# Cross-attention loop: keys, x, queries and mask rows prepared two batches early, long jobs on odd visits of three units

## The reference

```python
x = x + _L1_xattn_ref(_layernorm(x, axis=-1), ctx_1024, ctx_1024, mask_BxSxS2_if1, Wq, bq, Wk, bk, Wv, bv, Wo, bo)

def _L1_xattn_ref(Q, K, V, mask, Wq, bq, Wk, bk, Wv, bv, Wo, bo):
    q = _split_heads(Q @ Wq.T + bq)
    k = _split_heads(K @ Wk.T + bk)
    v = _split_heads(V @ Wv.T + bv)
    scores = jnp.einsum('bhqd,bhkd->bhqk', q, k) / jnp.sqrt(jnp.float32(D_K))
    scores = jnp.where(mask[:, None, :, :] == 0, NEG_INF, scores)
    attn = jax.nn.softmax(scores, axis=-1)
    out = jnp.einsum('bhqk,bhkd->bhqd', attn, v)
    ...
    return out @ Wo.T + bo
```

## Time and profile before

| | |
|---|---|
| time, median of 3 runs | 2673.34 us (2672.87 to 2675.73) |
| the profiled execution | 2665.32 us, span 2663.6 us |
| cross stage, set-up | 998 to 1074 us |
| cross stage, eight batches | 1074 to 1678 us |
| TensorE busy over the span | 2122.1 us (80%) |
| VectorE, ScalarE, GpSimd busy | 56%, 35%, 31% |
| mean granted TensorE clock | 0.937 |

### The profile page before, as it was taken

One profiled execution on the slowest core, in us unless ns is written; L12 is line 12 of the kernel. 1 busy time (PEld: TensorE's weight loads), 2 busy tenths in 40 slices (PEclk: granted clock), 3 DMA queues, 4 the chain that ended last, 5 costly groups with the idle time before them and its releaser, 6 DMA issues. The chain is left out here.

```text
span 2663.6 us, 37640 instructions
## 1 busy us (share of the span) xinstructions
PE 2122.1 (80%) x11952; PEld 1389.3 (52%) x11961; DVE 1484.3 (56%) x2297; ACT 926.3 (35%) x1539; POOL 836.8 (31%) x753
## 2 busy tenths in 40 slices
PE   2340899999999505889888888838999999999997
PEld 1340899999999502333333333614545545554554
DVE  7820454545554344567666666544656656656655
ACT  2410333333333200455555555312333333333332
POOL 0067553435550362122212222011323323333232
PEclk9999999999999856899999999669999999999999
DMA  3162332333322332232232232324233223223322
GB/s 126 63 243 101 111 115 79 117 122 110 122 78 65 109 88 88 89 102 89 82 104 84 87 98 86 118 53 95 58 73 86 65 68 86 69 61 86 76 56 64
DMA packets 149071, 244.68 MB, mean 92 GB/s; under 512 B 22502, under 2 KB 71310, under 8 KB 146698
## 3 DMA queue, kind: packets, MB, share of 16 engines
q1 hardware_dynamic: 109762, 164.07, 21.9%
q0 software_dynamic: 11104, 44.06, 4.8%
q10 hardware_dynamic: 28160, 35.99, 4.2%
HBM read 120.48 MB, written 67.04 MB: 70 GB/s over the span
## 5 line engine op out<-in xcount | busy, mean ns | idle before, releaser
L1108 DVE TENSOR_REDUCE ca_negmax<-ca_na 128x2 f32<-128x1024 f32 x272 | 332.4, 1224 | 153.6 <-PE ca_na L901 153.6
L1020 ACT ACTIVATE ca_pr<-ca_st 128x512 f32<-128x512 f32 x512 | 278.9, 597 | 206.6 <-PE ca_st L915 205.6
L901 PE MATMUL ca_na<-ca_k_stack,ca_q_stack 64*128 64x512 f32 x544 | 222.7, 489 | 59.0 <-DMA ca_q_stack<-ca_zrow 55.6
L592 DVE TENSOR_TENSOR ex_h<-ex_up,ex_sg 128x512 f32<-128x512 f32 x136 | 94.1, 692 | 306.8 <-ACT ex_sg L555 197.4
L1706 DVE TENSOR_REDUCE sa_negmax<-sa_na 128x1 f32<-128x512 f32 x272 | 182.7, 674 | 130.8 <-PE sa_na L1527 126.5
L915 PE MATMUL ca_st<-ca_q_stack,ca_k_stack 64*128 64x512 f32 x512 | 210.6, 473 | 29.5 <-ACT ca_pr L1020 26.5
L515 PE MATMUL ex_gp<-ex_xp,moe_gu_p 128*128 128x256 f32 x1632 | 221.8, 286 | 1.4 <-DVE ex_xp L578 1.4
L515 PE MATMUL ex_up<-ex_xp,moe_gu_p 128*128 128x256 f32 x1632 | 218.4, 284 | 0.0
L528 PE MATMUL ex_yp<-moe_dn_p,ex_hp 128*128 128x256 f32 x1632 | 208.8, 286 | 11.3 <-DVE ex_hp L582 11.3
L515 PEld LDWEIGHTS ex_gp<-ex_xp,moe_gu_p 128*128 128x128 f32 x1632 | 206.1, 193 | 2.4 <-DVE ex_xp L578 1.8
L528 PEld LDWEIGHTS ex_yp<-moe_dn_p,ex_hp 128*128 128x128 f32 x1632 | 198.8, 192 | 15.2 <-DVE ex_hp L582 15.2
(11 more groups left out here) (261 smaller groups left out, 3798.1 us busy)
## 6 DMA issues: line engine op xcount, KB each, us to landing
sa_q<-sa_qh SPq DMA_DIRECT2D x140, 128.0 KB
sa_k<-sa_kh SPq DMA_DIRECT2D x140, 128.0 KB
ex_raw_m<-masks ACTq DMA_DIRECT2D x34, 512.0 KB, 3.8
moe_gu_raw<-gateupT POOLq DMA_DIRECT2D x8, 2048.0 KB, 8.2
ca_q_stack<-q_parts SPq DMA_DIRECT2D x216, 64.0 KB
ca_k_stack<-k_parts SPq DMA_DIRECT2D x216, 64.0 KB
expert_rows<-rt_zeros SPq DMA_DIRECT2D x20, 512.0 KB, 15.9
k_parts<-ca_kp SPq DMA_DIRECT2D x9, 1024.0 KB, 4.3
```

What stands on the lines that cost most here:

```text
L901: last = pe.matmul(na[r % 2][:, i, :], q_stack[g][rows, i, t * P:(t + 1) * P], k_stack[g][rows, i, :], start=not masked, stop=True)
L1020: act.activation(pr[:, s // HG % 2, s % HG, :], st[s % 2][:, :], ACT.Exp, scale=DK ** -0.5).then_inc(exp_done, 1)
L1108: dve.tensor_reduce(negmax[:, g % 2, 1 - r % 2, :, r // 2], na[r % 2][:, :, :], AX.X, ALU.max, negate=True).then_inc(max_done, 1)
```

## The change

k, xT, q and rv are now made in batch b for batch b+2, v still for batch b+1 (`batch`). The stores of both k and q move to the end of SyncE's loop body, behind the loads of stack 3 and a wait for all four stacks. `ctxT` serves v alone and is loaded at the head of the body; k gets its own copy of the context, `ctxK`, loaded there too. The transposed mask has three buffers. Stack 0 waits only for unit 0 and for stores issued a batch earlier. The long jobs stand on odd visits of units 1 to 3 (three, three and two), none in unit 0. Before the loop the list `FIRST` makes k, x, q and rv of batch 0 and of batch 1, the latter behind v1.

```diff
-        JOBS = [("m", 0, 0), ("k0", 0, 1), ("n0", 0, 2), ("k1", 0, 3), ("xT0", 0, 4), ("xT1", 0, 5), ("rv", 0, 6), ("q0", 0, 7),
+        JOBS = [("m", 0, 0), ("n0", 0, 3), ("xT0", 0, 4), ("t0", 0, 5), ("xT1", 0, 6), ("t1", 0, 7),
+                ("m", 1, 0), ("v0", 1, 1), ("n1", 1, 2), ("o0", 1, 3), ("v1", 1, 5), ("rv", 1, 7),
...
-        FIRST = ["k0", "k1", "xT0", "xT1", "rv", "q0", "q1", "v0", "v1", "m"]
+        FIRST = [("k0", 0), ("k1", 0), ("xT0", 0), ("xT1", 0), ("rv", 0), ("q0", 0), ("q1", 0), ("v0", 0), ("v1", 0),
+                 ("xT0", 1), ("xT1", 1), ("rv", 1), ("k0", 1), ("k1", 1), ("q0", 1), ("q1", 1), ("m", 0)]
...
+        def batch(name, b):
+            return b + 1 if name[0] == "v" else b + 2
...
+            load_context(sp, io, ctxK, ck_in, 1)
+            load_bias_T(0, 0)
+            load_bias_T(1, 1)
             load_bias(0, 0)
...
             for g in range(G):
                 load_stack(g)
-            sp.wait_ge(misc_full, FIRST.index("v1") + 1)
-            load_context(sp, io, ctxT, ctx_in, 1)
+            for g in range(G):
+                sp.wait_ge(stack_in[g], LOAD)
+            store(kp, k_parts, misc_free, k_stored, first("k1", 1) + 1)
+            store(qp, q_parts, qp_ready, q_stored, 2 * KC)
             send_rows(0, 0)
             with sp.Fori(0, B) as b:
                 sp.wait_ge(exp_done, b * G * SLOTS + 2)
-                for g in range(G):
-                    sp.wait_ge(stack_in[g], b * LOAD + LOAD)
-                load_bias(nxt(b), (b + 1) % 2)
+                load_bias((b + 1) % B, (b + 1) % 2)
+                load_bias_T((b + 2) % B, (b + 2) % 3)
+                load_context(sp, io, ctxT, ctx_in, (b + 1) % B)
+                load_context(sp, io, ctxK, ck_in, (b + 2) % B)
                 send_rows(1, b * G + 1)
-                store(kp, k_parts, misc_free, k_stored, b * nj + (nf + number("k1") + 1))
-                send_rows(2, b * G + 2)
-                store(qp, q_parts, qp_ready, q_stored, b * KC + 2 * KC)
                 for g in range(G):
                     sp.wait_ge(exp_done, b * G * SLOTS + ((g + 1) * SLOTS + 2))
...
                     load_stack(g)
-                    if g == 1:
-                        send_rows(3, b * G + 3)
-                    if g == 2:
-                        load_context(sp, io, ctxT, ctx_in, (b + 2) % B)
-                        send_rows(0, b * G + 4)
+                    if g < G - 1:
+                        send_rows((g + 2) % G, b * G + (g + 2))
+                for g in range(G):
+                    sp.wait_ge(stack_in[g], b * LOAD + 2 * LOAD)
+                store(kp, k_parts, misc_free, k_stored, b * nj + (nf + number("k1") + 1))
+                store(qp, q_parts, qp_ready, q_stored, b * KC + 3 * KC)
...
@@ prepare (TensorE)
                 if name == "rv":
-                    pe.wait_ge(nbT_in, b * 16 + 16)
+                    pe.wait_ge(nbT_in, 32 if isinstance(b, int) else b * 16 + 16)
...
+                    now = isinstance(b, int) and b == 0
+                    if now:
+                        pe.wait_ge(ctx_in, 16)
+                    else:
+                        pe.wait_ge(ck_in, b * 16)
...
                 else:
+                    pe.wait_ge(ctx_in, b * 16 + 16)
...
@@ ScalarE, loop
+                        for n, name in jobs_at(g, r):
+                            if name[0] in "kxmt":
+                                evacuate(b * nj + (nf + n), name, batch(name, b))
                         if r == 0:
                             take(u, b * nj + nf + (number(f"n{g - 1}") + 1 if g else 0))
-                        for n, name in jobs_at(g, r):
-                            if name[0] in "kxmt":
-                                evacuate(b * nj + (nf + n), name, b + 1)
...
@@ GpSimd, loop
                     if g == 1:
-                        split_q(1, b * nj + (nf + number("q1")), b + 1)
                         add_bias(b)
-                    if g == 0:
-                        split_q(0, b * nj + (nf + number("q0")), b + 1)
-                    for i in {2: (0, 1), 3: (2,)}.get(g, ()):
-                        move_values(i, u + (G - g + i), b * nj + (nf + number("v1")))
+                    if g:
+                        move_values(g - 1, u + G - 1, b * nj + (nf + number("v1")))
+                    if g == 3:
+                        for c in range(KC):
+                            split_q(c, b * nj + (nf + number(f"q{c}")), b + 2)
...
@@ VectorE
+                if (name, b) == ("xT0", 1):
+                    normalise(1, 1)
...
-                        if (g, r) == (0, 1):
-                            normalise(b + 1, (b + 1) % B)
+                        if (g, r) == (0, 0):
+                            normalise(b + 2, (b + 2) % B)
```

More of the change, by code:

```diff
@@ L716, in cross_attention @@
         set_up = m.sem("set_up")
[L717 removed]
+        nb_in, nbT_in, ck_in = m.sem("nb_in"), m.sem("nbT_in"), m.sem("ck_in")
         xn_ready = m.sem("xn_ready")
@@ L751, in number, with first @@
             return next(n for n, j in enumerate(JOBS) if j[0] == name)
-        def nxt(b):
-            return b + 1 if isinstance(b, int) else (b + 1) % B
+        def first(name, b):
+            return FIRST.index((name, b))
+        def batch(name, b):
+            return b + 1 if name[0] == "v" else b + 2
         @block.sync
@@ L867, in prepare @@
                 if name == "rv":
-                    pe.wait_ge(nbT_in, b * 16 + 16)
+                    pe.wait_ge(nbT_in, 32 if isinstance(b, int) else b * 16 + 16)
                     for t in range(TB):
-                        last = pe.matmul(misc[:, :], tiny16[:, :], nbT[:, b % 2, t, :], start=(t == 0), stop=(t == TB - 1))
+                        last = pe.matmul(misc[:, :], tiny16[:, :], nbT[:, b % 3, t, :], start=(t == 0), stop=(t == TB - 1))
                 elif name[0] == "k":
-                    pe.wait_ge(ctx_in, b * 16 + 16)
+                    now = isinstance(b, int) and b == 0
[3 more added lines that the diff above has]
+                        pe.wait_ge(ck_in, b * 16)
                     for i in range(KC):
-                        last = pe.matmul(misc[:, :], wk[:, i, c * P:(c + 1) * P], ctxT[:, i, :], start=(i == 0), stop=(i == KC - 1))
+                        last = pe.matmul(misc[:, :], wk[:, i, c * P:(c + 1) * P], (ctxT if now else ctxK)[:, i, :], start=(i == 0), stop=(i == KC - 1))
                 elif name[0] == "x":
@@ L958, in all_units @@
                                 else:
-                                    prepare(job, name, b + 1)
+                                    prepare(job, name, batch(name, b))
             pe.wait_ge(w_in, 16 * 8)
-            for n, name in enumerate(FIRST[:-1]):
-                if n == 0:
-                    pe.wait_ge(set_up, SETUP)
-                prepare(n, name, 0)
+            pe.wait_ge(set_up, SETUP)
+            for n, (name, b) in enumerate(FIRST[:-1]):
+                prepare(n, name, b)
             for t in range(TB - 1):
@@ L1075, in _ @@
             for c in range(KC):
-                split_q(c, FIRST.index(f"q{c}"), 0)
+                split_q(c, first(f"q{c}", 0), 0)
             for g in range(G - 1):
-                move_values(g, g, FIRST.index("v1"))
+                move_values(g, g, first("v1", 0))
+            for c in range(KC):
+                split_q(c, first(f"q{c}", 1), 1)
             split_rows(nf - 1, 0)
```

27 lines of the change are left out of this document (16 added, 11 removed), and 5 rows, old and new, of the table JOBS.

## The result

The changed kernel takes 2690.57 us (median of 7 runs, 2684.43 to 2692.99) where the kernel before takes 2675.40 beside it (7 runs, 2668.72 to 2679.33): a ratio of 1.0057 with the interval 1.0043 to 1.0071, some 15 us slower. Forecast was no change (2673). The changed kernel's profiled execution has a span of 2690.4 us against 2663.6.

The account below looks back on a forecast made before the run. TensorE's cross loop was taken as the bound, with waits for late stacks; -7.7 - 12.2 + 16.4 + 3.5 = 0.0 us on the profiled 2665.3, whose median stands 8.0 above: 2673 us, no change; range 2635 to 2694.

Parts of the forecast that it names:

- (a): Cross loop, unit 2: stack 0 needs no fresh store, so its wait and the slow clock behind go, 8.4 us a batch.
- (b): Jobs in new places, without late transfers: units of 15.0, 17.35, 16.85 and 15.1 us, sum 64.3; places worth 2.4 a batch.
- (c): SP's queue: unit 1's rows behind 4.19 MB land at +22.3; batch 74.05 against 75.15, -7.7 us over batches 1 to 7.
- the 0.35 us: Unit 0's end: time from the last bulk byte at +21.95 to the rows landed with their completion at +22.3.
- The bounds (+20.5 to +23.8): Range for the rows' landing after unit 0's start: batch 72.2 to 75.6 us, batches 1 to 7 together -21 to +3.
- The estimate by the fit of the Trainium skill: 2.0 us plus bytes over 436 GB/s: 4.19 MB in 9.6 us, not 11.75, making the kernel 15 us faster; not used.
- (d): Batch 0 of the cross loop: no wait for rows, 66.0 us after against 78.2 before, -12.2 us.
- (e): Set-up before the loop: added jobs of batch 1, mostly at half clock, start the loop 16.4 us later, bounds 11 and 20.
- (f): The end: SP's last work includes both stores and their landing, 17.2 us against 13.7, +3.5.
- (C): Rival, chance 0.18: backlog flows slower, rows land past +23.4; at 300 GB/s +24.8, batch 76.55, whole 2694 us.
- (B): Rival, chance 0.15: rows overtake the bulk, landing at +17.3; batch 67.6 to 70 us, whole 2628 to 2645.
- The prediction's signs: Right: seven waits of 6 to 8 us for rows at unit 1's start; wrong: 2 to 3 (B), over 9 (C), none.

Follow-up runs that it names:

- e2_rows_ctx_first: Changed kernel with unit 1's rows issued first at a batch's head, ctxT right behind, then stack wait, both stores and other loads: 2599.18 us, ratio 0.9731 to before.
- e1_rows_first: Changed kernel with unit 1's rows issued first at a batch's head, then stack wait, both stores and the four loads: 2645.01 us, ratio 0.9905 to before.
- e13_hold_stack: Changed kernel with stack 0's fourteen loads held back until unit 1's rows have landed: 2678.44 us, ratio 1.0008 to before.
- e3: Changed kernel without the load of nb (512 KB) in the loop: 2670.65 us, ratio 1.0002 to before.
- e4_rows_act: Changed kernel with unit 1's four row transfers issued from ScalarE's queue in visit 3 of unit 0, bulk left on SyncE's: 2636.76 us, ratio 0.9870 to before.
- e12: Changed kernel without the load of ctxK in the loop (524 KB): 2671.80 us, ratio 1.0010 to before.
- e10_stores_rows: Changed kernel with batch head ordered stack wait, k and q stores, unit 1's rows, then the four loads: 2639.54 us, ratio 0.9887 to before.
- e6_loads_rows_stores: Changed kernel with batch head ordered four loads, unit 1's rows, then stack wait and both stores: 2616.08 us, ratio 0.9801 to before.
- e8_loads_then_stores: Changed kernel with batch head ordered stack wait, four loads, both stores, unit 1's rows last: 2671.92 us, ratio 1.0009 to before.

## Why the prediction was wrong

(a) *The late stack goes, 8.4 us a batch.* Right: no wait for a stack in 1170 to 1690, and unit 2 is 16.92 at clock 1.00. Batch 0 has no late rows, and there the gain of this and of the new places of the jobs stands alone: 78.4 to 66.3.

(b) *Units of 15.0, 17.35, 16.85, 15.1, sum 64.3.* Right: 64.2 to 65.2 in batches 1 to 6 of e2_rows_ctx_first, though unit 0 takes 16.1 in three of them (see the last section). In the changed kernel unit 1 takes 18.5 to 20.0 (forecast 17.35 + 2.45 = 19.8 with the slow clock after the wait), units 2 and 3 16.9 and 14.9.

(c) *The rows queue behind 4.19 MB and land at +22.3.* This is the term that failed. That the rows stand behind the bulk holds: their packets move at +22.0, and e1_rows_first takes the wait away by their place. The landing was off by 26.0 - 22.3 = 3.7 us. The last bulk byte was forecast for +21.95, and e13_hold_stack shows it, but for a few packets, at +22.2. The step that failed is the 0.35 us from there to PE's start. It is 1.6 when nothing else is queued, and 3.8 as the kernel was: the stack 0 loads, which my sum didn't hold at all, are worth the 2.2 us between. No row stood behind the 0.35, and one could have been read: in the trace of the kernel before, the rows of unit 1 take 1.2 us from the end of their last packet to the last step of their semaphore. With 1.6 the landing is +23.55 and the whole some 9 us more, about 2682 (an estimate). Units 1 to 3 gave back 0.5 and 0.2, so a batch came 3.1 dearer than forecast, and seven 21.7. The bounds (+20.5 to +23.8) took in the first of the two errors only. I took bytes over rate as the time of the last small transfer; the rate says when the bulk has flowed, and the row's landing is a term of its own.

The estimate by the fit of the Trainium skill ("DMA: Bandwidth & Descriptors", "Anatomy of one DMA") was misread beside it: 9.6 us is the bytes' part alone, and with the 2.0 us that the fit adds it is 11.6, as good as the 11.75 and not 15 us faster in all.

(d) *Batch 0, -12.2.* -12.1.

(e) *Set-up, +16.4, bounds 11 and 20.* +11.3, at the lower bound. The order of the added jobs was right, their clock was not. PE in the set-up of the changed kernel, with the earlier trace rows beside it:

```profile
1054.22 3.78 PE L893 MATMUL ca_misc<-ca_ctxK,cross_wk 128*128 128x512 f32 x4 [0.79 <-DVE ca_rv L1139]
1059.63 1.98 PE L893 MATMUL ca_misc<-ca_ctxK,cross_wk 128*128 128x512 f32 x4 [1.63 <-DVE ca_kp L1135]
1063.25 1.98 PE L900 MATMUL ca_misc<-ca_xT,cross_wq 128*128 128x512 f32 x4 [1.63 <-DVE ca_kp L1135]
1066.08 1.98 PE L900 MATMUL ca_misc<-ca_xT,cross_wq 128*128 128x512 f32 x4 [0.85 <-DVE ca_qf L1143]
```

Only k0 ran at the half clock (3.78 us), k1, q0 and q1 at the full one (1.98). From the end of v1 to the last values it is 25.0 us where the prediction had 28.2: 3.2 of the 5.1 us of the miss. Another 1.2 lie ahead of it, since batch 0's jobs (k0 to v1) took 29.7 us and not the 30.9 of the kernel before, as its half-speed stretches fell on other jobs, and 0.7 behind it, in the scores. Part of this is chance: the same set-up code takes 75.4 to 79.5 us in e3, e4, e12 and e13, where the changed kernel's profile has 77.6. By luck this miss hid a quarter of what (c) cost.

(f) *The end, +3.5.* +2.5.

Of the rivals, (C) is the one that came: a backlog that lands past +23.4. Its batch of 76.55 and its 2694 are near the 77.1 and 2690.6 measured, by luck: it had all bytes go at 300 GB/s, and they didn't. (By its own terms it lands at 9.3 + 0.9 + 14.0 + 0.35 = +24.5, and not at +24.8.) The chance of 0.18 was too low for it, since the forecast's own margin to the cross-over was 1.1 us, with a completion time that was read from no row. (B), rows that overtake the bulk, is refuted for one queue; with two, one row transfer overtook the stores in three batches of e4_rows_act.

The prediction's signs called waits of 6 to 8 us right and over 9 (C); they were 9.2 to 11.7.

## What to carry over

When a change makes an engine's operands earlier, look at the queue behind which the next small, urgent transfer stands, count the bytes ahead of it, and ask whether each of them is as urgent. Here the change gained 8.4 us a batch at one wait and lost more at another, by four 4 KB transfers behind 4.19 MB; sending the urgent ones first (rows, then ctxT, then stores and the rest) gives 2599 us without touching a single job of the engines. Give a small transfer behind bulk the time of the bytes plus one to two microseconds, and two more where loads like the stack's are issued right behind it: so it was here.

## What the runs showed of the hardware

- Stack loads issued behind the rows on the same queue delayed TensorE's release by 2.2 us (26.0 to 23.8, e13_hold_stack) and made its time uneven (25.4 to 26.5 against 23.64 to 23.87). Most of it lies behind the rows' data: from their last packet to the last step of their semaphore it took 2.4 to 3.5 us in the three kernels with stack 0's loads right behind, and 0.9 to 1.5 us in five kernels with stores, bulk loads or nothing there. The stack's loads are 64 KB each, in packets of 2 KB; such a packet took 205 ns on the mean (1259.6 to 1263 in the changed kernel), where one of the bulk of the same size took 90 (1255.1 to 1259). They moved at 133 to 172 GB/s with a full DMA share (1 us windows behind the bulk in e2_rows_ctx_first and e10_stores_rows) where the bulk moves at 380. Why they are slow, and why the rows' semaphore waits for them, is not shown; the traces don't tell the sixteen engines apart.
- Where stores give way to loads in one queue (the changed kernel and e13_hold_stack, after some 2 MB), two windows of 1 us fall to 184 to 244 GB/s, at a cost of 0.9 us. From loads to stores e6_loads_rows_stores shows nothing (381, 399 and 414 GB/s). The low windows inside the loads of e8_loads_then_stores are not explained.
- A 4 KB row transfer on ScalarE's queue passed stores queued on SP's: its packets moved at +11.5 to +12.1 while these flowed at 348 to 393 GB/s from +9.9 on, where without them they moved at +10.2 (e4_rows_act, batches 1, 2 and 5 against 3, 4, 6 and 7).
- Unit 0 without a long job is not always at full clock although TensorE waits for nothing long: in e2_rows_ctx_first it takes 14.8 us in four of seven batches and 16.1 in the other three. Parts of such a unit 0 (batch 3) and of one at full clock (batch 2), in the columns of the earlier trace rows:

```profile
1279.51:1283.51 4.00, 3.18 (x17) 1.24 (x17) 3.77 (x7) 3.83 (x8) 1.36 (x3) 1.00 0.36 93
1283.51:1288.51 5.00, 4.88 (x22) 1.94 (x24) 2.86 (x3) 2.71 (x6) 1.51 (x5) 0.66 0.31 86
1215.15:1219.15 4.00, 3.18 (x17) 1.24 (x17) 3.77 (x7) 3.83 (x8) 1.36 (x3) 1.00 0.37 97
1219.15:1224.15 5.00, 4.88 (x32) 1.86 (x32) 4.19 (x6) 3.73 (x8) 1.51 (x5) 1.00 0.31 83
```

  In batch 3 TensorE is busy 3.18 us of 4.00, and the granted clock falls to 0.66 over the next 5 us. The last two rows are the same stretches of batch 2: the same 3.18 us busy, and the clock stays at 1.00. So what TensorE did just before does not tell the two apart, and the cause is open. It costs 1.3 us a time, 4 in all. Whether a long job moved back into unit 0 would keep the clock up was not tried.
- From the rows' last packet to the last step of their semaphore it took 0.4 us where the four transfers stood alone (e1_rows_first, e2_rows_ctx_first), and 1.2 us in the kernel before, where they moved together behind 1 MB. Left open is what makes the difference, and the 0.6 us by which taking nb away shortens unit 0 beyond its bytes.
